# First key group of an attention stage: later query parts on GpSimd, later key products one step later, doubled output weights copied earlier

## The reference

```python
x = x + s * g                              # layer 0: scan, experts
xn = _layernorm(x)
q = (xn @ Wq.T).reshape(b, s, 32, 64)      # rope on q and k
k = (xn @ Wk.T).reshape(b, s, 8, 64)
v = (xn @ Wv.T).reshape(b, s, 8, 64)
logits = q k^T / sqrt(64), causal
out = softmax(logits) v                    # each key head serves 4 query heads
s = out @ Wo.T
g = silu(sign-weight product of sign(norm(xn)))
x = x + s * g
```

## Time and profile before

| | |
|---|---|
| Three runs | 753.35 us median (749.12 to 753.63) |
| The profiled execution | 748.34 us, of which the span from first to last instruction is 746.5 us |
| TensorE busy | 688.0 us, 92% of the span |
| VectorE, ScalarE, GpSimd busy | 510.5, 442.0, 385.2 us |
| Mean granted TensorE clock | 0.993 of full speed |

### The profile page before, as it was taken

One profiled execution on the slowest core, in us unless ns is written; L12 is line 12 of the kernel. 1 busy time (PEld: TensorE's weight loads), 2 busy tenths in 40 slices (PEclk: granted clock), 3 DMA queues, 4 the chain that ended last, 5 costly groups with the idle time before them and its releaser, 6 DMA issues.

```text
span 746.5 us, 13408 instructions
## 1 busy us (share of the span) xinstructions
PE 688.0 (92%) x4447; PEld 598.2 (80%) x4448; DVE 510.5 (68%) x1072; ACT 442.0 (59%) x1075; POOL 385.2 (52%) x434
## 2 busy tenths in 40 slices
PE   2999999999999999699879999999999999999976
PEld 2887998989889898587668888888888878787864
DVE  7483556434333245897878878888888888887765
ACT  4435343332341432448786787778877788878772
POOL 1403342432224312235765797777877788777540
PEclk9899999999999999999999999999999999999999
DMA  8165877787778755226533332343324423242011
GB/s 293 44 217 170 286 240 241 252 261 229 247 234 251 214 170 163 43 76 191 147 109 79 93 82 65 95 93 83 85 65 102 93 66 87 58 110 58 1 29 57
DMA packets 108453, 102.25 MB, mean 137 GB/s; under 512 B 51104, under 2 KB 78688, under 8 KB 108256
## 3 DMA queue, kind: packets, MB, share of 16 engines
q1 hardware_dynamic: 106272, 95.62, 44.8%
q0 software_dynamic: 2112, 5.77, 2.4%
HBM read 69.24 MB, written 11.14 MB: 108 GB/s over the span
## 4 chain that ended last, share of the span: by engine, by line
PE 65%; DVE 20%; ACT 6%; issue 5%; POOL 2%; DMA 1%; SPq 1%; DVEq 0%; ACTq 0%
PE bank L1700 14%; PE bank L1734 8%; PE bank L1556 7%; PE bank L1873 5%; DVE p_lo L1071 3%; PE bank L1840 3%; DVE o_rest L1080 3%; PE bank L1560 3%; DVE nmax L1062 3%; PE bank L1561 3%; PE bank L1562 3%; PE bank L1841 2%; DVE q_mix L1028 2%; DVE q_mix L1029 2%; PE bank L1884 2%
## 5 line engine op out<-in xcount | busy, mean ns | idle before, releaser
L1518 POOL TENSOR_TENSOR prob<-prob,rinv 128x128 f32<-128x128 f32 (+3 forms) x256 | 176.6, 722 | 89.2 <-DVE rinv L1067 89.2
L1322 ACT ACTIVATE prob<-bank,nmax 128x512 f32<-128x512 f32 (+3 forms) x256 | 133.2, 526 | 42.3 <-DVE nmax L1062 30.7
L1071 DVE TENSOR_TENSOR p_lo<-bank,p_hi 128x512 fp32r<-128x512 f32 x160 | 109.5, 685 | 58.0 <-ACT p_hi L1329 55.9
L1329 ACT ACTIVATE p_hi<-bank 128x512 fp32r<-128x512 f32 x160 | 95.4, 596 | 44.1 <-PE bank L1556 43.1
L1700 PEld LDWEIGHTS bank<-xgT,wm 128*128 128x128 f32 x920 | 108.7, 192 | 4.5 <-issue 2.9
L1700 PE MATMUL bank<-xgT,wm 128*128 128x128 f32 x920 | 111.3, 275 | 0.5 <-ACT xgT L1234 0.5
L1840 PE MATMUL bank<-kT,qT 128*128 128x512 f32 (+3 forms) x256 | 83.4, 331 | 19.8 <-ACT prob L1322 15.3
L1556 PE MATMUL bank<-cst,prob 128*128 128x128 f32 x640 | 96.6, 273 | 3.2 <-ACT prob L1322 2.5
L1062 DVE TENSOR_REDUCE nmax<-bank 128x1 f32<-128x512 f32 (+2 forms) x192 | 91.3, 502 | 2.8 <-PE bank L1843 2.6
L1873 PE MATMUL bank<-p_lo,v_parts 128*128 128x256 f32 (+3 forms) x288 | 91.7, 341 | 0.1
L1491 POOL DMA_INDIRECT y_rows<-y_row,to_row x21 | 22.8, 1084 | 118.2 <-DVE y_row L931 92.5
(11 more groups left out here) (310 smaller groups left out, 1517.9 us busy)
## 6 DMA issues: line engine op xcount, KB each, us to landing
wm<-in_w_moe SPq DMA_DIRECT2D x23, 1280.0 KB
wm<-in_w_moe SPq DMA_DIRECT2D x23, 640.0 KB, 5.1
qT<-q_hi SPq DMA_DIRECT2D x124, 64.0 KB, 2.0
qT<-q_lo SPq DMA_DIRECT2D x124, 64.0 KB, 2.0
wo_twice<-wo_hi SPq DMA_DIRECT2D x32, 128.0 KB, 2.5
k_exp<-k_rows SPq DMA_DIRECT2D x56, 64.0 KB, 2.0
wtl<-in_w_moe_tail SPq DMA_DIRECT2D x46, 64.0 KB
y_rows<-gate SPq DMA_DIRECT2D x1, 2048.0 KB, 13.8
```

The source lines that it names most:

```text
L1071: TT(p_lo[:, b_, :], bank[2 + b_ % 2][:, :], p_hi[:, b_, :].bitcast(F32), ALU.subtract).then_inc(plo_done, 1)
L1322: ins = actv(prob[:, i % 2, h, POFF[j]:POFF[j] + (j + 1) * P], bk[:, at:at + (j + 1) * P], ACT.Exp, bias=nmax[:, i % 2, h, j:j + 1], accum ...
L1329: actv(p_hi[:, b_, :], bank[2 + b_ % 2][:, :], ACT.Copy).then_inc(phi_done, 1)
L1518: ins = GT(seg, seg, rinv[:, i % 2, k, j:j + 1].to_broadcast([P, (j + 1) * P]), ALU.mult)
```

## The change

Three things are changed, all in the first group. `half_first` ends with `l(i,0)` and `l(i,1)` on GpSimd at step n + 4, place 6, in place of `ql` on VectorE at step n + 4, place 3.3; that concerns i = 2 and 3 (i = 1 keeps `ql`). `KW` goes from step 2 to step 1, and every `Kq`, `Kr` and `Ka` goes one step later. In SyncE's queue `double_wo(0)` stands ahead of the second store of the later keys.

```diff
--- before.py
+++ after.py
@@ -91,7 +91,7 @@
 
     def half_first(i, n):
         z = [(n, 8, "Q", i, 0), (n + 1, 8, "Q", i, 1), (n + 1, 8, "r", i, 0), (n + 2, 8, "r", i, 1)]
-        return z + [(n + 2, 8.1, "qa", i, 0), (n + 3, 4.5, "h", i, 0), (n + 4, 3.3, "ql", i, 0)]
+        return z + [(n + 2, 8.1, "qa", i, 0), (n + 3, 4.5, "h", i, 0), (n + 4, 6, "l", i, 0), (n + 4, 6, "l", i, 1)]
 
     def half(i, n, slow):
         z = [(n, 8, "Q", i, 0), (n + 1, 8, "Q", i, 1), (n + 1, 8, "r", i, 0), (n + 2, 8, "r", i, 1), (n + 3, 6, "a", i, 0),
@@ -100,11 +100,11 @@
 
     ready = [(11, 8, "Kh", 2, 0), (12, 6, "Kl", 2, 0)]
     if kind == "first":
-        ready += [(2, 7, "KW", 0, 0), (3, 0, "VQ", 0, 0)] + half_first(2, 7) + half_first(3, 13)
+        ready += [(1, 7, "KW", 0, 0), (3, 0, "VQ", 0, 0)] + half_first(2, 7) + half_first(3, 13)
         ready += [(0, 1, "r", 1, 0), (0, 8, "r", 1, 1), (1, 8, "qa", 1, 0), (2, 4.5, "h", 1, 0), (3, 3.3, "ql", 1, 0)]
         ready += [(t - TB, 8, "V", t, 0) for t in range(TB, NT)]
         for b in range(BATCH):
-            n = 4 + 7 * b
+            n = 5 + 7 * b
             for k in range(2):
                 ready += [(n + k, 8.2, "Kq", b, k), (n + k + 1, 8.2, "Kr", b, k), (n + k + 4, 6.2, "Ka", b, k)]
         ready += [(8 + t, 8.95, "F", t, 0) for t in range(NT)]
@@ -641,10 +641,10 @@
             load_wq(2)
             store_k(1, 0)
             move_q(1, 0)
+            double_wo(0)
             store_k(1, 1)
             spread_k(1, 1)
             load_v(1, 1)
-            double_wo(0)
             load_wo(1)
 
             def group(g, more):
```

## The result

The changed kernel took 758.27 us (median of 14 runs, 755.18 to 760.07), the kernel before in the same series 749.31 us (14 runs, 747.54 to 753.76). The medians lie 9.0 us apart. The ratio, which is worked out over the executions and is not the quotient of the medians, is 1.0109, 95% interval 1.0089 to 1.0130: 8.2 us slower, between 6.7 and 9.7. The profiled execution took 757.06 us with a span of 755.3 us, against 748.34 and 746.5 before. Of the executions in this document two were far longer than the rest (1377.97 us in experiment 1, 979.18 us in experiment 11); the medians have them in, the ratios do not.

A forecast was written before the change was run, and what follows sets the result against it. TensorE's idle time in the first group, about 8 us, was taken as the only room. Terms 0, +7.0 (0.94 inside) and -0.9 gave +6.1, called +6.0; on the 753.35 us median that is 759.4 us, range 752.5 to 762.5.

The forecast's parts named there:

- the order conflict: First group: Q(3,0) and Q(3,1) wait for Kr(1,0) and Kr(1,1), now behind other VectorE work; +7.0 us.
- the clock rival: TensorE's clock falls in the gap ahead of Q(3,0), costing about 1.5 us more: +7.6, 761 us; chance 0.18.
- the store rival: The later keys' store, held back on SyncE, costs the second group: +8 to +9, 762 us; chance 0.07.
- signs of being wrong: Q(3,0) waits under 3 us, the later stretch absorbs over 2 us, or the granted clock drops there.
- Part 1: KW earlier, later keys' first half later: wk_lo's 1.4 us wait goes, an exponential comes late; 0, between -1.4 and +0.9.
- Part 2: Lower query parts on GpSimd relieve VectorE: E(2,2) 0.94 us earlier; qa(2) without Ka overlap gives E(2,0) -0.6.
- Part 3: Later keys' second half: Q(3,0) waits 4.8 us, Q(3,1) about 3.5, both for Kr; +7.0 us at Q(3,1).
- Nothing caught up: None of the +7.0 us comes back by the group's end; the rival, part caught up, had +2 to +4, chance 0.17.
- Part 4: double_wo earlier on SyncE: W's 0.9 us wait goes, -0.9; the store slips to about 391, costed at 0.

The follow-up runs named there:

- experiment 1: The changed kernel with all later keys' steps (Kq, Kr, Ka) put back where they were: 745.65 us, ratio 0.9947 to the kernel before.
- experiment 11: The kernel before with nine useless matmuls in TensorE's 2.46 us gap ahead of the last stage: 749.62 us, ratio 1.0012 to the kernel before.
- Experiment 3: The changed kernel with 18 useless matmuls ahead of Q(3,0) and 12 ahead of Q(3,1): 756.69 us, ratio 1.0096 to the kernel before.
- experiment 8: The kernel before with only KW moved, to step 1: 749.79 us, ratio 1.0005 to the kernel before.
- experiment 2: The changed kernel with only the second half of the later keys (Kq, Kr, Ka(1,k)) put back: 746.56 us, ratio 0.9960 to the kernel before.
- experiment 6: The kernel before with only the lower query parts moved to GpSimd (two l for ql, i = 2 and 3): 749.08 us, ratio 1.0004.
- experiment 5: The kernel before with only the later keys' move one step later (n = 5 + 7 * b): 758.97 us, ratio 1.0129 to the kernel before.
- experiment 9: The changed kernel with Kr at the head of its step, restoring VectorE's earlier order: 749.23 us, ratio 0.9997 to the kernel before.
- experiment 4: The changed kernel with Q, r, h and l of i = 3 one step later too: 751.17 us, ratio 1.0023 to the kernel before.
- experiment 7: The kernel before with only double_wo(0) put ahead of the store: 748.50 us, ratio 0.9991 to the kernel before.
- experiment 10: The changed kernel with the later keys put back and Kr ahead of its step's p_lo on VectorE: 744.81 us, ratio 0.9941 to the kernel before.
- the third series: The kernel before, unchanged, run beside the last four follow-up kernels: 748.48 us.

## Why the prediction was right, and where its sizes were off

**The forecast** was 759.4 us, +6.0 from the order conflict, within 752.5 to 762.5. The median is 758.27. The mechanism was the forecast's, in its place; the clock rival came true on top of it. Experiment 3 separates them: without the clock's fall the stretch is +6.0.

**That the time came so near is luck.** Two errors offset each other. The forecast stood on 753.35 us, the median of three runs, where 14 runs beside the changed kernel gave 749.31, 4.0 less. And the change was taken 3.0 too small: it is +9.0 by the medians, +8.8 in the profiles, 8.2 by the ratio, above the forecast's own +4.5 to +7 and the +7.6 of the clock rival. Seen from 749.31, the same sum gives 755.3, and the range, moved down by 4.0, would end at 758.5, just above what was measured. The +8 to +9 of the store rival fits as a number, but not as a cause: nothing waited behind the store, and from the first `sT` copy to the end the kernel takes 354.6 us, against 354.7 before. Of the prediction's own signs of being wrong one came true: the granted clock dropped. The second group began 10.0 us later, not 6 to 7.

- **Part 1** (0, between -1.4 and +0.9). The wait for `wk_lo` became 1.63 us for an exponential and 0.64 for N, as described. KW alone gains 0.6 at S(2,2) (experiment 8), the first half's move costs 0.9 (2 against 1). S(2,2) came 0.4 late, 0.14 of which is the later start of the group. Right within its bounds.
- **Part 2** (0.94). E(2,2) came 0.97 us earlier in experiment 6. The Trainium skill (SBUF — State Buffer, section "SBUF: two separate sides") states a port shared by VectorE and GpSimd, which only one of them can hold at a time. The traces agree: `qa(2)` took 1.84 us beside GpSimd's Ka and 1.23 without it, and `kT` 2.13 and 2.14 us beside `ql` and 1.26 and 1.29 without it. But the 0.6 us gained on `qa(2)` show up in no earlier S(2,2): the late first half took them.
- **Part 3** (+7.0). Kr(1,0) was put at 369.75 and stood at 370.15, Q(3,0) at 371.1 and stood at 371.49, both 0.4 late as S(2,2) was. The waits were called 4.8 and 3.5 us and are 4.81 and 3.28. From Q(3,0) to S(2,4) the sum took 2.9 us and it was 4.69: +1.8 for the clock. 7.0 + 0.4 + 1.8 is the measured +9.2 at Q(3,1). Experiments 1, 2, 5 and 9 show that the conflict on VectorE is the cause, and 9 that the later products on TensorE are 1.7 us of the loss.
- **Nothing caught up**, as taken: from +9.6 at S(3,0) the delay went to +10.0.
- **Part 4** (-0.9). Right: +10.0 at the second group and +9.0 at W. The store went to 395.5, not 391, with Ka(1,1) at 394.23, behind l(3,0) and l(3,1) at 391.76 and 393.00; still nobody waited for what stood behind it.
- **What it had wrong is the clock**, a term that the sum left out: "gaps of 2.29 us left the clock at 1.00" with "It decides between 2.3 and 5.7 us of idle time", and the price of 1.5 us. The clock fell behind both gaps, not one, and cost 2.7 us (experiment 3): 1.8 behind the first, where the rival had about 1.5, and 0.9 behind the second. And no such point was found: it fell behind gaps of 1.81 us in experiment 4, 2.22 in 5 and 2.26 in 7 and 8, and stood behind one of 3.28 us in 5. The row that I set against the rival was one execution, and worth less than I gave it.

## What to carry to other kernels

When one list of steps orders all engines, moving a product also moves its consumer in another engine's queue; look first at who waits for the consumer's release of the bank, and move product and release apart if need be (experiment 9: 9.8 us of the stretch back with one number). An edit that loses can hide others that gain: the other parts of this change together were worth 3.3 us by the medians. A forecast of a difference should be checked as a difference: a base of three runs was off by 4.0 us here, almost half of the effect. What 1 us in the trace brings can be taken away by a clock that falls in one execution and not in the next, so compare a stretch of the trace and not only medians, and look for falls of the clock within the stretch.

## What the runs showed of the hardware

- **The same gap lets TensorE's clock fall in some executions.** Behind the 2.46 us gap ahead of the last stage it stayed at 1.00 in six of the twelve profiles that have it unfilled, and was 0.50 in the other six (experiments 3, 4, 6 to 9), for 1.5 us of span (354.6 to 354.7 us from the first `sT` copy to the end against 356.1 to 356.6). Behind Q(3,0)'s wait of 2.26 to 2.29 us it stayed in before and in experiment 11, and fell in 7 (1.2 us) and 8. In queries later it fell behind 1.81 us, in keys alone behind 2.22 us; behind Q(3,0)'s 1.60 to 1.61 us it stood in experiments 1, 2, 6 and 9. Behind the 5.72 us ahead of the group it was low in every profile, but the fall came at different times in that same wait, 2.3 us (experiment 4) to 5.2 us (before, experiment 10) after TensorE had gone idle. That these falls make up the scatter between executions is suggested by the third series: of 27 executions of the kernel before, the 14 with a span up to 746.7 us have a mean clock of 0.990 to 0.993, the 13 from 747.8 on 0.985 to 0.988. It isn't shown one by one, as only profiled executions have windows. What decides in a single execution stays open. The Trainium skill (TensorE: Matmul & The Clock Gate, "Part 1: The HAM clock gate") says that the gate's timing runs freely and does not start anew with the kernel. The different times of the fall in the same wait fit that; that it decides the other cases is not shown.
- **The clock fell behind a gap of 1.10 us in two profiles.** In experiment 11 (the gap ahead of it filled) and in 10 (unfilled, clock at 1.00 behind it) the clock fell behind the wait of W some 16 us later; in the other twelve it stood there. So filling one gap kept the clock up there and did not show in the time; filling the two of the changed kernel took 2.7 us off the stretch.
